# Building one-hot routing tables in bfloat16, one column of the top-6 at a time, in a decoder kernel

## The reference, cut to what matters

```
scores = softmax(x @ w_router.T)              # 1024 x 64
topw, topi = top_k(scores, 6)
combine[token, expert] = topw where chosen, else 0
routed = sum over experts of combine[:, e] * swiglu(x, wg[e], wv[e], wo[e])
x = layernorm(x + routed + swiglu(x, swg, swv, swo))
```

## Time and profile before

| | us |
|---|---|
| median of the 3 executions | 1339.24 |
| lowest and highest | 1335.9 and 1339.72 |
| the profiled execution | 1340.74 |
| its span, first to last instruction | 1338.8 |

### The profile page before, as it was taken

The page is one execution under the profiler, slowest core; times in us unless marked ns, Lnnn a source line. Parts: engine busy times, 40 slices in busy tenths (PEclk is TensorE's granted clock), DMA queues, the critical chain, the costliest instruction groups (busy, mean ns, idle before and its releaser), DMA issues.

```text
span 1338.8 us, 18300 instructions
## 1 busy us (share of the span) xinstructions
PE 1005.0 (75%) x5543; PEld 641.3 (48%) x5543; DVE 856.5 (64%) x1402; ACT 495.6 (37%) x847; POOL 378.9 (28%) x325
## 2 busy tenths in 40 slices
PE   6698888888888888844698888872078577778665
PEld 2466465555555555533566555540036343444333
DVE  5556767667676758596745433325767899464766
ACT  2543333434343333431123323330322443677264
POOL 0133434444444343551124333316700000000000
PEclk8689998989898989876899999995579775898777
DMA  4902020111111111002248777763210100000000
GB/s 139 312 23 81 17 73 25 61 37 51 47 51 47 51 47 39 32 1 84 77 138 250 241 248 243 244 197 98 85 47 19 45 0 0 1 0 0 0 1 32
DMA packets 54930, 106.63 MB, mean 80 GB/s; under 512 B 7433, under 2 KB 27537, under 8 KB 54385
## 3 DMA queue, kind: packets, MB, share of 16 engines
q1 hardware_dynamic: 49329, 90.99, 20.5%
q0 software_dynamic: 5568, 15.21, 4.0%
HBM read 86.61 MB, written 19.56 MB: 79 GB/s over the span
## 4 chain that ended last, share of the span: by engine, by line
issue 32%; PE 18%; DVE 18%; POOL 13%; SPq 11%; ACT 3%; DMA 3%; another core or an unknown queue 0%; DVEq 0%; POOLq 0%; ACTq 0%
POOL drive L1124 6%; POOL state L1130 5%; SPq L519 5%; DVE row_max L2000 2%; PE ps L964 2%; SPq L516 2%; SPq L525 2%; POOL y L1133 2%; SPq L522 2%; PE ps L1007 2%; PE ps L979 1%; PE ps L802 1%; POOL yg L1180 1%; DVE stats L1554 1%; DVE x_den L2027 1%
## 5 line engine op out<-in xcount | busy, mean ns | idle before, releaser
L1130 POOL TENSOR_TENSOR state<-state,c_row 128x1024 f32<-128x1024 f32 x32 | 75.4, 2355 | 306.6 <-DVE state L1549 306.6
L617 PE MATMUL ps<-w_vg,xT 128*128 128x512 f32 x256 | 137.2, 686 | 29.8 <-DVE th L1573 29.7
L802 PE MATMUL ps<-w_gv,xgT 128*128 128x352 f32 x272 | 97.1, 488 | 26.6 <-DMA w_gv<-in_w_gv 25.7
L1549 DVE TENSOR_TENSOR_SCAN state<-decay,drive 128x1024 f32<-128x1024 f32 x32 | 87.5, 2735 | 32.2 <-POOL drive L1124 32.2
L617 PEld LDWEIGHTS ps<-w_vg,xT 128*128 128x128 f32 x256 | 52.3, 216 | 102.9 <-DVE th L1573 52.4
L1124 POOL TENSOR_TENSOR drive<-du,b_row 128x1024 f32<-128x1024 f32 x32 | 82.2, 2578 | 58.4 <-DVE y L1691 58.4
L572 PE MATMUL ps<-xT,w_qks 128*128 128x512 f32 x192 | 93.1, 639 | 0.0
L1560 DVE TENSOR_TENSOR aT<-ps,tri 128x768 f32<-128x768 f32 x64 | 59.2, 954 | 47.6 <-PE ps L582 47.6
L1164 POOL DMA_INDIRECT xg<-x_dram,tok_cur x68 | 66.2, 974 | 53.6 <-issue 20.4
L2000 DVE TENSOR_REDUCE row_max<-ps 128x1024 f32 x64 | 74.1, 1216 | 7.7 <-PE ps L979 7.0
L1798 DVE SCALAR_TENSOR_TENSOR g_th<-g_th,ps 128x176 f32<-128x176 f32 x76 | 25.6, 337 | 82.7 <-ACT g_th L1209 72.0
(11 more groups left out here) (291 smaller groups left out, 2239.3 us busy)
## 6 DMA issues: line engine op xcount, KB each, us to landing
w_gv<-in_w_gv SPq DMA_DIRECT2D x68, 352.0 KB
w_dn<-in_w_dn SPq DMA_DIRECT2D x68, 176.0 KB
y_dram<-y_out SPq DMA_DIRECT2D x68, 128.0 KB
b_row<-x_dbl_dram SPq DMA_DIRECT2D x16, 512.0 KB, 3.7
c_row<-x_dbl_dram SPq DMA_DIRECT2D x16, 512.0 KB, 5.4
y_dram<-blank SPq DMA_DIRECT2D x2, 3584.0 KB, 22.5
w_vg<-in_wvg SPq DMA_DIRECT2D x8, 512.0 KB, 3.4
w_qks<-in_wqks SPq DMA_DIRECT2D x8, 384.0 KB, 2.9
```

The source lines that it names most:

```text
L617: last = mm(bank(PJ + t % 2), xT[:, k, t * P:(t + 1) * P], w_vg[:, k, :], start=(k == 0), stop=(k == KD - 1))
L802: last = mm(ps[:, 2 * j + 1, 0:2 * F], x_of(k), w[:, k, :], start=(k == 0), stop=(k == KD - 1))
L1130: G.tensor_tensor(state[:, n % 2], state[:, n % 2], c_row[:, j], ALU.mult).then_inc(read_out, 1)
L1549: V.tensor_tensor_scan(state[:, n % 2], decay[:, n % 2], drive[:, n % 2], 0.0, ALU.mult, ALU.add).then_inc(scanned, 1)
```

## The change

The tables become bfloat16 and are built choice by choice. For each tile and each of its six choices VectorE issues three `tensor_scalar` instructions, which read one tensor, a bfloat16 copy of `iota`, and take the row's or the block's number as one value per partition. One value of a bfloat16 holds whole numbers exactly only in part of the range of the token numbers, so the token number t*128 + partition is kept in two parts, each in a table of its own: the partition number (`tok_id[:, 0:1]`) and t*128. The matmul has both as its 224 moving columns, and at the end the two halves of the bank are added: one is copied to SBUF (`tok_high`), and the sum of the other and it is written to `tok_of`. The copy of `iota` is made once, after `norm(1)`, behind a wait for `moe_consts`.

```diff
@@ memory
-        row_hot = sb("row_hot", [P, 2, TOPK, P])
-        blk_hot = sb("blk_hot", [P, 2, TOPK, NBLK])
+        iota_bf = sb("iota_bf", [P, P], BF16)
+        row_hot = sb("row_hot", [P, 2, TOPK, P], BF16)
+        blk_hot = sb("blk_hot", [P, 2, TOPK, 2, NBLK], BF16)
+        tok_high = sb("tok_high", [P, NBLK])
@@ TensorE
-                last = mm(ps[:, Y + 1, 0:NBLK], row_hot[:, t % 2, k, :], blk_hot[:, t % 2, k, :], start=(n == 0),
+                last = mm(ps[:, Y + 1, 0:2 * NBLK], row_hot[:, t % 2, k, :],
+                          blk_hot[:, t % 2, k].rearrange("p a n -> p (a n)"), start=(n == 0),
                           stop=(n == TILES * TOPK - 1))
@@ VectorE, after norm(1)
+            dve.wait_ge(moe_consts, 64)
+            then(V.tensor_copy(iota_bf[:], iota[:]))
             dve.wait_ge(route_mm, 1)
@@ VectorE, for t in range(TILES)
-                V.tensor_tensor(row_hot[:, t % 2], iota[:].unsqueeze(1).to_broadcast([P, TOPK, P]),
-                                slot_row[:, t, :].unsqueeze(2).to_broadcast([P, TOPK, P]), ALU.is_equal)
-                then(V.tensor_tensor(blk_hot[:, t % 2], iota[:, 0:NBLK].unsqueeze(1).to_broadcast([P, TOPK, NBLK]),
-                                     slot_blk[:, t, :].unsqueeze(2).to_broadcast([P, TOPK, NBLK]), ALU.is_equal))
-                V.tensor_scalar(blk_hot[:, t % 2], blk_hot[:, t % 2], tok_id[:, t:t + 1], None,
-                                ALU.mult).then_inc(hot_ready, 1)
+                for k in range(TOPK):
+                    row, blk = slot_row[:, t, k:k + 1], slot_blk[:, t, k:k + 1]
+                    V.tensor_scalar(row_hot[:, t % 2, k], iota_bf[:], row, None, ALU.is_equal)
+                    V.tensor_scalar(blk_hot[:, t % 2, k, 0], iota_bf[:, 0:NBLK], blk, tok_id[:, 0:1], ALU.is_equal, ALU.mult)
+                    last = V.tensor_scalar(blk_hot[:, t % 2, k, 1], iota_bf[:, 0:NBLK], blk, float(t * P), ALU.is_equal,
+                                           ALU.mult)
+                last.then_inc(hot_ready, 1)
             dve.wait_ge(hot_used, TILES)
-            V.tensor_copy(tok_of[:], ps[:, Y + 1, 0:NBLK]).then_inc(tok_known, 1)
+            then(V.tensor_copy(tok_high[:], ps[:, Y + 1, NBLK:2 * NBLK]))
+            V.tensor_tensor(tok_of[:], ps[:, Y + 1, 0:NBLK], tok_high[:], ALU.add).then_inc(tok_known, 1)
```

## The result

The changed kernel takes 1349.41 us (median of four, 1347.78 to 1350.26) where the kernel before takes 1337.96 (median of four, 1335.9 to 1339.72). The ratio is 1.0082, with a 95% interval of 1.0066 to 1.0098. The forecast was 1348.9, slower by 0.7%. By the ratio the change costs 11.0 us (8.8 to 13.1), by the two medians 11.5; the forecast was 9.7.

A forecast was written before the change was run, and what follows sets the result against it. VectorE was taken to set the pace of the tables, by 0.65 us a tile. +8.0 - 0.3 + 0.3 + 1.7 = +9.7 us on 1339.24 gave 1348.9 us; own range 1346 to 1352, 8 in 10 for 1344 to 1355.

The forecast's parts named there:

- VectorE's part: Building the tables on VectorE: 144 small instructions at 558 ns a choice, 26.9 us in place of 18.9, +8.0 us.
- A per-partition scalar: In the tables' VectorE instructions: each value read per partition costs 59 ns, paid in full from start to start.
- The overlap: Between successive VectorE instructions in the tables: each starts 85 ns before the one ahead of it ends.
- the fixed part: Cost of each VectorE instruction in the tables regardless of its columns: 162 ns, read from float32 rows.
- One of the prediction's signs of being wrong: In the profile of VectorE's tables: durations above 280 ns with one value would show the forecast's column rate wrong.
- TensorE's last tile: TensorE's matmuls for the last tile of the tables: 1.3 us in place of 1.6, -0.3 us.
- The sum at the end: After the tables: a PSUM copy and an addition in place of one cast of 0.29 us, +0.3 us.
- The copy of iota: The bfloat16 copy, about 0.23 us, costs nothing because VectorE stands idle 5.04 us there for the router's matmuls.
- The clock: TensorE's clock stays low through the tables and 3.8 us of dense work at the shared expert's start, +1.7 us.
- The delay reaches the end: Behind the tables: a later tok_known counts in full to the end of the kernel.
- The rival of an absorbed delay: Behind the tables, a weight's or gather's transfer ends last anyway and takes up the delay: about 1340 us, chance 0.05.
- The rivals of rate: Tables' bfloat16 instructions run at 0.52 ns a column (1353.3 us, chance 0.12) or 1.03 (1361.9 us, chance 0.05), not 0.26.

The follow-up runs named there:

- with constants: Changed kernel with constants in place of every per-partition scalar, both tables zero, so only the tables' stage is read: 0.298 us a choice against 540 ns.
- the changed kernel's second execution: The changed kernel run once more, unchanged, against the kernel before: ratio 1.0068 (1.0042 to 1.0093), four runs.
- the fillers: Changed kernel plus six unread bfloat16 matmuls of 512 columns before TensorE's wait for each tile but the first: ratio 1.0043 to the kernel before.
- the float32 source: Changed kernel with the three instructions reading float32 iota, still writing bfloat16: 0.632 us a choice, 0.092 more than with the bfloat16 source.
- the last experiment: Changed kernel with large bfloat16 comparisons, choice innermost, low part multiplied on ScalarE, four table copies, TensorE warmed up: ratio 0.9979 to the kernel before.

## Why the prediction was right

The direction and the place were right, and so was each sign. Two terms were mis-sized by 0.9 us each, in opposite directions: VectorE's part came out smaller and the clock's larger. That the sum of 9.7 meets the stage's 9.8 so closely is luck. So is part of the 0.5 us between 1348.9 and 1349.41: the forecast started from a median of 1339.24 for the kernel before, which came out at 1337.96 beside the changed one.

*VectorE's part, forecast +8.0, measured +7.1* (26.0 - 18.9), or 540 ns a choice for 558. A per-partition scalar costs 60 ns from start to start (forecast 59). The rate is 0.26 ns a column: 327 ns for 672 columns with a constant and 183 for 112. The overlap is that of the forecast, too: with constants the three instructions last 186 + 183 + 183 = 552 ns and take 298, 85 off each; in the changed kernel's second execution they last 245 + 301 + 242 = 788 ns and take 540, 83 off each. The term that was mis-sized is the fixed part. It was read as 162 ns from float32 rows, and is 183 - 112 x 0.26 = 154 here. The forecast durations of 254, 309 and 250 ns are 8 to 9 ns too long each, 25 ns a choice, of which the overlap takes back 7.

One of the prediction's signs of being wrong did come up: durations above 280 ns with one value. In the changed kernel's trace their medians are 300 and 298. They grew while the starts kept their distance, and the second execution has 245 and 242 with the same 540 ns a choice, so a duration is no safe sign of the column rate here; the distance of the starts is.

*TensorE's last tile, forecast -0.3:* from the end of the last `blk_hot` at 666.16 to the copy at 667.54, 1.4 us; before 1.7 (659.91 to 661.58). Right. *The sum at the end, +0.3:* two instructions, 667.54 to 668.13, 0.6 for 0.3. Right. *The copy of iota, nothing:* it lasts 0.23 us, and VectorE still idles 4.97 us behind it.

*The clock, forecast +1.7, measured +2.6* (7.58 - 4.97). The mechanism was named and is shown by the fillers: clock full, 4.97 us. The size was read from the first tile of the tables, where the clock rose after 3.8 us; here it rose after about 5.2 (668.3 to 673.5), where three to four were forecast, within the bounds. In the other kernels with a low clock behind the tables the same records took 6.4 to 7.9 us, so this term can't be read from one place in a trace to better than about a microsecond. The half clock's share of the loss, 46%, held: 5.2 x 0.46 = 2.4.

*The delay reaches the end.* It is 9.8 us at the first turned rows and 9.9 at the end of the span. The rival of an absorbed delay is excluded.

*The rivals of rate.* The 0.52 and 1.03 are excluded: by the changed kernel's starts, and by the float32 source, which runs at 0.52 and is 92 ns a choice slower.

The measured ratio gives 11.0 us (8.8 to 13.1), the stage 9.8. The forecast of 9.7 and the stage lie in that interval.

On the Trainium skill's figure of 58 cycles (VectorE: DVE Perf Modes, section The TRN2 errata): an estimate by it is 13.1 us for the 144 instructions, and they took 26.0. Even with constants, 0.298 us a choice, they take 14.3. The trace agrees with the advice in the same section of the Trainium skill to make tiles of 512 elements or more: in float32 and with one token number, two small instructions a choice took 22 us where the three large ones a tile took 18.9.

## What to carry to other kernels

Price a small VectorE instruction by its start-to-start time with all that it reads: here 0.10 us with constants, of which the columns are 0.03, and 0.06 more for every per-partition scalar. The narrower type saved only on the columns. Before making an off-path engine's work cheaper, look at what its clock does: TensorE's cheaper matmuls were hidden, and behind them its clock was at half for 5.2 us of the work that was not. When a step moves to a third engine, count the loop through all of them against the number of buffers.

## What the runs showed of the hardware

The clock fell on a TensorE whose record shows it busy: in the last experiment 5.00 of 5.00 us busy from 650 to 655, at 0.50, after 1.00 from 641 to 645. Its matmuls there read operands with a stride of six elements and took 0.30 us each at either level of the clock. VectorE and ScalarE had finished with the tables by 650.7 and the pace of the matmuls stayed, so their reads of the same memory are not the cause. That the stride is the cause is argued, not shown, since no run changed it alone.

Durations of back-to-back small VectorE instructions drift while their starts don't: in the changed kernel's trace `row_hot` lasts 0.26 us at 640.13 and 0.36 at 665.41, every choice taking 0.54; in its second execution all lie between 242 and 254 ns.

ScalarE's multiplication of 672 float32 columns by a per-partition scale takes 0.86 us (the runs with the multiplication on ScalarE), and the same in bfloat16 0.86 (the last experiment), so bfloat16 saved nothing there.
